# Attention scores on 32-row instead of 64-row TensorE tiles

## The chip, the cores and the metric

The kernel runs on one core of a Trainium2 chip. The metric is the device time of one execution in microseconds (us), the median of three runs.

## What is computed

For an input of 8 sequences with 1024 tokens of 128 channels the kernel normalizes each token (layer norm) and adds to the input an 8-head attention and a mixture of experts of the normalized tokens. In the attention a head has 2 query and key channels and 16 value channels:

```python
q = (x @ Wq.T + bq).reshape(B, M, H, dqk)      # dqk = 2
k = (x @ Wk.T + bk).reshape(B, M, H, dqk)
v = (x @ Wv.T + bv).reshape(B, M, H, dv)       # dv = 16
scores = jnp.einsum('bmhd,bnhd->bhmn', q, k) / math.sqrt(dqk)
scores = jnp.where(scores >= 0, scores, 0.2 * scores)
beta = jax.nn.softmax(scores, axis=-1)
out = jnp.einsum('bhmn,bnhd->bmhd', beta, v).reshape(B, M, C)
return gamma * out + x
```

The experts are 16 (12 of them two-layer networks with 512 hidden channels), with two chosen per token and a capacity of 1024 tokens each.

## The kernel before

The work has these stages on one core. First a prologue over 16 groups of 512 tokens (two of each sequence): statistics, normalizing, transposing, projecting to q, k, v and the router's logits, splitting q and k into three bfloat16 parts each (high, middle, low), and storing the parts to `parts_dram`. The groups are software-pipelined: each engine's program is a loop over steps, in which a step holds pieces of several groups. The parts lie in two buffers, so the copy of a group's high parts (line 674, ScalarE) waits until the stores of the group two before it have landed (`parts_out0`, `parts_out1`). Behind the last group VectorE ranks the tokens' experts. Then come attention on the first three sequences, the experts, and attention on the other five.

SP's queue in order: the loads of `x` (L261); eight DMAs of one row of -1 into `kz` (L269); twelve DMAs that clear `disp` (L272); for each group the stores of its parts (L281 once, L285 three times, L292 for a row of shifts); the operand loads of the first sequence (L312 to L314); and then, pass by pass, further operand loads and the moves of finished rows.

A score of one head is a product over 18 rows: 3 key parts times 3 query parts times 2 channels. The softmax is made safe by a bound, the shift, of each query; it is subtracted as one further row (query side: the shift; key side: -1). The raw product holds the 18 rows alone. VectorE rectifies it where it lies, in PSUM (L1133: maximum with 0, times 4), a second product, the shifted one, with the shift's row too, is added onto it there, and ScalarE takes the exponential to `pr` (L718).

A tile for one head pair has 64 rows: 18 for one head, 18 for the other head, zeros, and the two rows of ones at the end. `kz` holds the keys once for each of the two heads of a tile, with zeros in the other's rows; `q2` holds the queries of both. Two tiles, at rows 0 and 64, make the two heads of a unit.

Attention runs over 32 passes (sequence, group of 4 heads, half of the queries: 512), each of 16 units; a unit is 128 keys of two heads, so 1024 scores per partition in two PSUM banks. There are 512 units, and a ring of three such bank pairs. `unit_of` gives a unit its pass, block of keys (`kc`) and head pair. TensorE's order is written out by hand: for each unit i, `shifted(i)` (L835, waits for VectorE's rectification of i), `scores(i + 2)` (L825, the raw products, waits for the exponential of i - 1, which frees the ring's place), and `values` (L855), half of a value step, in four column tiles of 32. At each pass's sixth unit VectorE also transposes the last pass's result (L1109, L1115).

The changed names are `TILE`, `ONES` (the row of ones, and the rows of a raw product), `q2`, the row writes at L263 to L269, `load_operands` (L301 to L314), the clearing of `q2` (L397), `scores` and `shifted`.

Of the kernel before, what the change touches and what calls it, by code (L numbers as in the profile page):

```python
# [5 lines left out]
F32 = mybir.dt.float32  # L6
BF16 = mybir.dt.bfloat16
# [5 lines left out]
P = 128  # L13
B, M, C = 8, 1024, 128
# [3 lines left out]
H, DV, DQ = 8, 16, 2  # L18
HG = 4
NHG = H // HG  # L20
# [4 lines left out]
HALF = 512  # L25
# [3 lines left out]
PROWS = KROW + 3 * QP  # L29
NPROD = 3 * 3 * DQ  # L30
NROW = NPROD + 1
TILE = 64
ONES = TILE - 2
DIRS = 16
E, E_MLP, FFN = 16, 12, 512
FC = FFN // P
# [16 lines left out]
PAIRS = HG // 2  # L53
# [48 lines left out]
def build(nc, x, consts, w_qk, b_qk, w_vr, b_v, r_b, n_w, n_w_row, w1t, b1, w2t, b2, cvec, gamma, out):  # L102
    parts_dram = nc.dram_tensor("parts_dram", [2, NROW * H, T], BF16, kind="Internal").ap()
# [3 lines left out]
    with ExitStack() as ctx:  # L107
        def sb(name, shape, dt=F32):
            return ctx.enter_context(nc.sbuf_tensor(name, shape, dt))

        def sem(name):
            return ctx.enter_context(nc.semaphore(name))
# [33 lines left out]
        shift = sb("shift", [P, GW], BF16)  # L146

        kz = sb("kz", [P, NHG, PAIRS, M], BF16)
        q2 = sb("q2", [P, NHG, M], BF16)
        w1 = sb("w1", [P, 4 * FFN])  # L150
        vp = sb("vp", [P, NHG, TB, HG, 32])
        pr = sb("pr", [P, BUFS, HG, HALF])
# [4 lines left out]
        rowones = sb("rowones", [1, M], BF16)  # L157
# [48 lines left out]
        S = {n: sem(n) for n in names}  # L206
# [6 lines left out]
        def wait_done(engine, name, count):  # L213

            if not (isinstance(count, int) and count <= 0):
                engine.wait_ge(S[name], count)
# [22 lines left out]
        def unit_of(i):  # L239

            p, n = divmod(i, UP)
            return p, p // NQ % NHG, p % NQ, n // PAIRS, n % PAIRS
# [7 lines left out]
        def spreads(p):  # L250

            return sum(k not in LAST and k % 2 == p % 2 for k in range(p + 1))

        def pass_at(b, hg, qh):
            return (b * NHG + hg) * NQ + qh

# [2 lines left out]
        def _(sp):  # L259
# [3 lines left out]
            sp.wait_ge(S["init_rdy"], 1)  # L263
            sp.wait_ge(S["ztile"], 1)
            sp.wait_ge(S["qz_init"], 1)
            for hg in range(NHG):
                for g in range(HG):
                    r = TILE * (g // PAIRS) + ONES + g % PAIRS
                    sp.dma_start(kz[r:r + 1, hg, g % PAIRS, :], rowones[:]).then_inc(S["kz_init"], 16)  # L269

            for e in range(E_MLP):
                sp.dma_start(disp[e * CAP:(e + 1) * CAP, :].rearrange("(p j) c -> p (j c)", p=P),  # L272
# [23 lines left out]
            for u in range(2):  # L296
                sp.wait_ge(S[f"parts_out{u}"], 64 * B)
                sp.wait_ge(S[f"shift_out{u}"], 16 * B)
            sp.wait_ge(S["kz_init"], 16 * NHG * HG)

            def load_operands(b, hg):  # L301

                if b > 0:
                    sp.wait_ge(S["s2"], UP * (pass_at(b - 1, hg, NQ - 1) + 1))
                for g in range(HG):
                    h = hg * HG + g
                    tok = bass.ts(b, M)
                    krows = parts_dram[1, :, tok].rearrange("(r h) t -> h r t", h=H)[h]
                    qrows = parts_dram[0, :, tok].rearrange("(r h) t -> h r t", h=H)[h]
                    r = TILE * (g // PAIRS) + NPROD * (g % PAIRS)  # L310
                    o = TILE * (g // PAIRS) + ONES + g % PAIRS
                    sp.dma_start(kz[r:r + NPROD, hg, g % PAIRS, :], krows[0:NPROD, :]).then_inc(S[f"ld{hg}"], 16)  # L312
                    sp.dma_start(q2[r:r + NPROD, hg, :], qrows[0:NPROD, :]).then_inc(S[f"ld{hg}"], 16)
                    sp.dma_start(q2[o:o + 1, hg, :], qrows[NPROD:NROW, :]).then_inc(S[f"ld{hg}"], 16)  # L314

            def store_sequence(s):

# [18 lines left out]
            def operands_in(p):  # L336

                if p % NPB == 0 and p > 0:
                    load_operands(p // NPB, 1)
                if p % NPB == NQ and p // NPB + 1 < B:  # L340
                    load_operands(p // NPB + 1, 0)

            for hg in range(NHG):
                load_operands(0, hg)
# [45 lines left out]
        def _(pool):  # L390
# [3 lines left out]
            pool.memset(va[:, :, :, DV:DV1], 1.0)  # L394
            pool.memset(vp[:], 0.0).then_inc(S["init_rdy"], 1)
            pool.memset(kz[:].rearrange("p a e m -> p (a e m)").bitcast(F32), 0.0)
            pool.memset(q2[:].rearrange("p a m -> p (a m)").bitcast(F32), 0.0).then_inc(S["qz_init"], 1)  # L397

            def prologue(at):
                if at(1):  # L400
# [22 lines left out]
            def value_rows(b, hg):  # L423

                if b > 0:
                    pool.wait_ge(S["pv"], TB * (pass_at(b - 1, hg, NQ - 1) + 1))
                pool.tensor_copy(vp[:, hg, :, :, 0:DV1],
                                 va[:, bass.ts(b, TB), hg * HG:(hg + 1) * HG, :]).then_inc(S["vp_rdy"], 1)
# [339 lines left out]
        def _(pe):  # L768
# [42 lines left out]
            for n, (lhs, rhs) in enumerate(((cbf[:, C_TRI:C_TRI + P], cnt), (onesb[:], incl))):  # L811
                pe.wait_ge(S["cnt_rdy"], n + 1)
                for half in range(2):
                    last = pe.matmul(ps_acc[:, half, :], lhs, rhs[:, half * HALF:(half + 1) * HALF], start=(n == 0),
                                     stop=(n == 1))
            last.then_inc(S["pos_rdy"], 1)

            def scores(i):
                p, hg, qh, kc, pair = unit_of(i)
                if i % (NQ * UP) == 0:  # L820
                    pe.wait_ge(S[f"ld{hg}"], NLOAD * (p // NPB + 1))
                wait_done(pe, "exps", i - RING + 1)
                for k in range(2):
                    r = TILE * k
                    last = pe.matmul(ring[i % RING][:, k, :], kz[r:r + ONES, hg, pair, kc * P:(kc + 1) * P],  # L825
                                     q2[r:r + ONES, hg, qh * HALF:(qh + 1) * HALF], start=True, stop=True,
                                     tile_position=(r, 0))
                last.then_inc(S["s1"], 1)

            def shifted(i):  # L830
                p, hg, qh, kc, pair = unit_of(i)
                pe.wait_ge(S["relu"], i + 1)
                for k in range(2):
                    r = TILE * k
                    last = pe.matmul(ring[i % RING][:, k, :], kz[r:r + TILE, hg, pair, kc * P:(kc + 1) * P],  # L835
                                     q2[r:r + TILE, hg, qh * HALF:(qh + 1) * HALF], start=False, stop=True,
                                     tile_position=(r, 0), skip_group_check=True)
                last.then_inc(S["s2"], 1)

# [29 lines left out]
            def ahead(b, n):  # L869

                for i in range(b * NUB, b * NUB + n):
                    scores(i)

            def attention(b0, b1):
                first, end = b0 * NUB, b1 * NUB
                for i in range(first, end):
                    shifted(i)
                    if i + AHEAD < end and i != BH * NUB:
                        scores(i + AHEAD)
                    if i > first + PAIRS:  # L880
                        values((i - 3) // PAIRS, (i - 3) % PAIRS)
                values((end - 3) // PAIRS, (end - 3) % PAIRS)
                if b1 == BH:
                    pe.wait_ge(S["exps"], end - RING + 1)
                    turn_rows(0, 0)
                for j in range(end - 2, end):
                    values(j // PAIRS, j % PAIRS)
# [333 lines left out]
```

## Time and profile before

| | |
|---|---|
| device time, median of 3 runs | 941.46 us (941.45 to 942.2) |
| span of the profiled execution | 940.0 us |
| TensorE matmul busy | 861.2 us (92%) |
| VectorE busy | 735.3 us (78%) |
| ScalarE busy | 691.3 us (74%) |
| GpSimd busy | 601.5 us (64%) |
| attention, first three sequences | 127 to 362 us |
| experts | 362 to 543 us |
| attention, other five | 543 to 931 us |

The profile is of one execution; its span runs from the program's first to its last instruction, and the device time also holds what lies around it, some 1.5 us. A matmul's busy time includes the latency of its pipeline, so a full TensorE row isn't TensorE at its peak. Idle time of an engine is put down to what ended it.

### The profile page before, as it was taken

What the parts mean: (1) busy time and instruction counts of PE and PEld (TensorE: products, weight loads), DVE (VectorE), ACT (ScalarE), POOL (GpSimd) and SP (SyncE); (2) the same over time, 40 slices, a digit from 0 to 9 for tenths busy, and PEclk for the clock granted to TensorE, in tenths of its full rate; (3) what the DMA queues carried; (4) which work ended last, traced back from release to release, by engine and by line L of the source; (5) the groups of instructions that cost most, each with busy time, mean ns of one, the idle gap of its engine ahead of it and who ended that gap; (6) DMA issues with size and microseconds to landing.
All of it is one profiled execution on the core that took longest, in us unless ns stands there. A gap on an engine that the chain in (4) does not pass through costs nothing. (4 is left out here: it accounts for less than half of the span.)

```text
span 940.0 us, 20061 instructions
## 1 busy us (share of the span) xinstructions
PE 861.2 (92%) x7499; PEld 348.9 (37%) x7500; DVE 735.3 (78%) x859; ACT 691.3 (74%) x811; POOL 601.5 (64%) x610
## 2 busy tenths in 40 slices
PE   0688269999999999999999999999999999999997
PEld 0444112222222224776867732222222222222222
DVE  5788889999999994101011099999999999999996
ACT  0578888888888887444453568888888888888886
POOL 3355247777777663999999226657567575765782
PEclk9999659999999999999999999999999999999999
DMA  7833101111111112233242210102112111210202
GB/s 214 303 66 74 32 27 33 51 40 51 47 27 36 25 38 88 90 121 116 93 138 71 94 44 22 40 19 59 36 25 59 25 36 29 70 29 13 69 18 55
DMA packets 71225, 59.36 MB, mean 63 GB/s; under 512 B 33770, under 2 KB 58178, under 8 KB 71136
## 3 DMA queue, kind: packets, MB, share of 16 engines
q1 hardware_dynamic: 61520, 48.06, 17.6%
q0 software_dynamic: 8192, 9.37, 3.6%
q8 instruction: 55, 0.90, 0.4%
q10 hardware_dynamic: 1424, 0.76, 0.3%
q14 instruction: 34, 0.28, 0.1%
HBM read 31.58 MB, written 30.02 MB: 66 GB/s over the span
## 5 line engine op out<-in xcount | busy, mean ns | idle before, releaser
L1133 DVE TENSOR_SCALAR ps<-ps 128x1024 f32<-128x1024 f32 x512 | 600.1, 1224 | 14.6 <-PE ps L825 11.7
L718 ACT ACTIVATE pr<-ps 128x1024 f32<-128x1024 f32 x512 | 523.4, 1023 | 104.5 <-PE ps L835 72.9
L855 PE MATMUL ps<-pr,vp 128*32 128x256 f32 x4096 | 327.2, 392 | 0.1
L835 PE MATMUL ps<-q,kz 64*128 64x512 bf16 x1024 | 200.7, 389 | 10.2 <-DVE ps L1133 4.4
L825 PE MATMUL ps<-q,kz 62*128 62x512 bf16 x1024 | 200.3, 389 | 2.9 <-DMA q<-parts_dram 1.3
L505 POOL DMA_INDIRECT xs<-eout,idxs x128 | 129.0, 1008 | 105.0 <-ACT pr L718 75.5
L490 POOL DMA_INDIRECT disp<-xn,idx x128 | 125.9, 984 | 50.8 <-issue 29.2
L835 PEld LDWEIGHTS ps<-q,kz 64*128 64x128 bf16 x1024 | 49.0, 93 | 225.7 <-DVE ps L1133 188.4
L1152 DVE TENSOR_TENSOR pr<-ps,parts 128x1024 f32<-128x1024 f32 x12 | 14.7, 1225 | 149.6 <-PE ps L920 149.6
L855 PEld LDWEIGHTS ps<-pr,vp 128*32 128x32 f32 x4096 | 81.1, 108 | 119.4 <-issue 117.6
L744 ACT ACTIVATE pr<-ps,b1s 128x512 f32<-128x512 f32 x96 | 65.8, 687 | 53.7 <-PE ps L909 53.7
L920 PEld LDWEIGHTS ps<-w,pr 128*128 128x128 f32 x768 | 88.6, 192 | 6.2 <-issue 6.2
L920 PE MATMUL ps<-w,pr 128*128 128x128 f32 x768 | 89.8, 275 | 0.0
L825 PEld LDWEIGHTS ps<-q,kz 62*128 62x128 bf16 x1024 | 49.3, 93 | 107.1 <-ACT pr L718 76.3
L909 PE MATMUL ps<-pr,w 128*128 128x512 f32 x192 | 84.7, 593 | 0.0
L628 POOL TENSOR_TENSOR y<-y,xn x24 | 56.4, 2351 | 4.9 <-POOL xn L625 4.9
L525 POOL TENSOR_TENSOR y<-y,xs 128x256 f32<-128x256 f32 x64 | 46.5, 727 | 11.4 <-POOL y L525 5.7
L452 POOL TENSOR_TENSOR y<-y,moved 128x256 f32<-128x256 f32 x32 | 23.4, 731 | 45.1 <-DMA moved<-att 26.8
L909 PEld LDWEIGHTS ps<-pr,w 128*128 128x128 f32 x192 | 35.5, 190 | 40.2 <-issue 39.5
L404 POOL TENSOR_TENSOR ot<-pr,parts 112x512 f32<-112x512 f32 x16 | 18.7, 1170 | 38.1 <-ACT parts L674 38.0
L737 ACT ACTIVATE pr<-ps,nw 128x512 f32<-128x512 f32 x24 | 15.2, 683 | 37.4 <-PE ps L898 37.4
L518 POOL TENSOR_TENSOR xs<-xs,co 128x256 f32<-128x256 f32 x64 | 37.9, 618 | 0.6
(122 smaller groups left out, 530.3 us busy)
## 6 DMA issues: line engine op xcount, KB each, us to landing
moved<-att SPq DMA_DIRECT2D x480, 8.0 KB
disp<-pr SPq DMA_DIRECT2D x12, 512.0 KB, 4.9
eout<-pr SPq DMA_DIRECT2D x12, 512.0 KB, 2.9
y<-in_x SPq DMA_DIRECT2D x8, 512.0 KB, 8.1
out<-y SPq DMA_DIRECT2D x7, 512.0 KB
w<-in_w1t SPq DMA_DIRECT2D x12, 256.0 KB, 3.2
w<-in_w2t SPq DMA_DIRECT2D x12, 256.0 KB, 3.4
xs<-disp SPq DMA_DIRECT2D x6, 512.0 KB, 4.9
```

What stands on the lines that cost most here:

```text
L490: pool.indirect_dma_start(out=disp, out_offset=bass.IndirectOffsetOnAxis(ap=idx[:, k, s * TB + t:s * TB + t + 1], axis=0), in_=xn[:, s * T ...
L505: pool.indirect_dma_start(out=g1[:, g % 2, t, c, :], out_offset=None, in_=eout, in_offset=bass.IndirectOffsetOnAxis(ap=idxs[:, c, GB * i + ...
L525: pool.tensor_tensor(yt, yt, rows[:, :, c, :], ALU.add).then_inc(S["comb" if c else "weighted"], 1)
L628: pool.tensor_tensor(yb, yb, xb, ALU.add).then_inc(S["pool_step"], 1)
L718: act.activation(pr[:, c % BUFS, 2 * pair:2 * pair + 2, :], ring[i % RING], ACT.Exp, scale=SLOPE).then_inc(S["exps"], 1)
L744: act.activation(hs[:, f, half * HALF:(half + 1) * HALF], ps[:, 2 + n % 4, :], ACT.Gelu, bias=b1s[:, u, f:f + 1]).then_inc(S["gel"], 1)
L825: last = pe.matmul(ring[i % RING][:, k, :], kz[r:r + ONES, hg, pair, kc * P:(kc + 1) * P], q2[r:r + ONES, hg, qh * HALF:(qh + 1) * HALF], ...
L835: last = pe.matmul(ring[i % RING][:, k, :], kz[r:r + TILE, hg, pair, kc * P:(kc + 1) * P], q2[r:r + TILE, hg, qh * HALF:(qh + 1) * HALF], ...
L855: last = pe.matmul(acc[p % 2][32 * g:32 * g + 32, cols], vp[:, hg, kc, g, :], pr[:, c % BUFS, g % PAIRS * 2 + g // PAIRS, cols], start=(kc ...
L909: pe.matmul(ps[:, 2 + n % 4, :], w1[:, 2 * u * FFN + f * P:2 * u * FFN + (f + 1) * P], dt_[:, half * HALF:(half + 1) * HALF], start=True, ...
L920: mm = pe.matmul(o, hs[:, f, j * P:(j + 1) * P], w1[:, (2 * u + 1) * FFN + f * P:(2 * u + 1) * FFN + (f + 1) * P], start=(f == 0), stop=(f ...
L1133: dve.tensor_scalar(s, s, 0.0, 1.0 / SLOPE - 1.0, ALU.max, ALU.mult).then_inc(S["relu"], 1)
```

## The change

Each head gets a tile of its own, of 32 rows: 18 rows, 13 rows of zeros, and the row of ones at the end. Four tiles fill the 128 rows: two sets of two. Both sets hold the same operands, the keys and queries of all four heads of the group, a head pair behind the other in the free dimension (so `q2` has a further dimension, of twice the size). A unit with an even block of keys uses the tiles at rows 0 and 32, one with an odd block those at 64 and 96. As a block has two units, unit i + 2 uses the other set than unit i.

The rows of ones are written by 16 DMAs instead of 8. The operand loads are 12 DMAs per sequence and head group as before; each now brings two heads, and each is made for both sets. `shifted` takes all 32 rows, `scores` the first 31. The order of instructions on TensorE stays.

```diff
--- before.py
+++ after.py
@@ -29,8 +29,9 @@
 PROWS = KROW + 3 * QP
 NPROD = 3 * 3 * DQ
 NROW = NPROD + 1
-TILE = 64
-ONES = TILE - 2
+TILE = 32
+ONES = TILE - 1
+SETS = 2
 DIRS = 16
 E, E_MLP, FFN = 16, 12, 512
 FC = FFN // P
@@ -146,7 +147,7 @@
         shift = sb("shift", [P, GW], BF16)
 
         kz = sb("kz", [P, NHG, PAIRS, M], BF16)
-        q2 = sb("q2", [P, NHG, M], BF16)
+        q2 = sb("q2", [P, NHG, PAIRS, M], BF16)
         w1 = sb("w1", [P, 4 * FFN])
         vp = sb("vp", [P, NHG, TB, HG, 32])
         pr = sb("pr", [P, BUFS, HG, HALF])
@@ -251,6 +252,10 @@
 
             return sum(k not in LAST and k % 2 == p % 2 for k in range(p + 1))
 
+        def rows_of(z, k):
+
+            return TILE * (2 * z + k)
+
         def pass_at(b, hg, qh):
             return (b * NHG + hg) * NQ + qh
 
@@ -263,10 +268,12 @@
             sp.wait_ge(S["init_rdy"], 1)
             sp.wait_ge(S["ztile"], 1)
             sp.wait_ge(S["qz_init"], 1)
-            for hg in range(NHG):
-                for g in range(HG):
-                    r = TILE * (g // PAIRS) + ONES + g % PAIRS
-                    sp.dma_start(kz[r:r + 1, hg, g % PAIRS, :], rowones[:]).then_inc(S["kz_init"], 16)
+            for z in range(SETS):
+                for k in range(2):
+                    r = rows_of(z, k) + ONES
+                    for hg in range(NHG):
+                        for pair in range(PAIRS):
+                            sp.dma_start(kz[r:r + 1, hg, pair, :], rowones[:]).then_inc(S["kz_init"], 16)
 
             for e in range(E_MLP):
                 sp.dma_start(disp[e * CAP:(e + 1) * CAP, :].rearrange("(p j) c -> p (j c)", p=P),
@@ -296,22 +303,22 @@
             for u in range(2):
                 sp.wait_ge(S[f"parts_out{u}"], 64 * B)
                 sp.wait_ge(S[f"shift_out{u}"], 16 * B)
-            sp.wait_ge(S["kz_init"], 16 * NHG * HG)
+            sp.wait_ge(S["kz_init"], 16 * NHG * SETS * HG)
 
             def load_operands(b, hg):
 
                 if b > 0:
                     sp.wait_ge(S["s2"], UP * (pass_at(b - 1, hg, NQ - 1) + 1))
-                for g in range(HG):
-                    h = hg * HG + g
-                    tok = bass.ts(b, M)
-                    krows = parts_dram[1, :, tok].rearrange("(r h) t -> h r t", h=H)[h]
-                    qrows = parts_dram[0, :, tok].rearrange("(r h) t -> h r t", h=H)[h]
-                    r = TILE * (g // PAIRS) + NPROD * (g % PAIRS)
-                    o = TILE * (g // PAIRS) + ONES + g % PAIRS
-                    sp.dma_start(kz[r:r + NPROD, hg, g % PAIRS, :], krows[0:NPROD, :]).then_inc(S[f"ld{hg}"], 16)
-                    sp.dma_start(q2[r:r + NPROD, hg, :], qrows[0:NPROD, :]).then_inc(S[f"ld{hg}"], 16)
-                    sp.dma_start(q2[o:o + 1, hg, :], qrows[NPROD:NROW, :]).then_inc(S[f"ld{hg}"], 16)
+                tok = bass.ts(b, M)
+                for k in range(2):
+                    heads = slice(hg * HG + k * PAIRS, hg * HG + (k + 1) * PAIRS)
+                    krows = parts_dram[1, :, tok].rearrange("(r h) t -> r h t", h=H)[:, heads, :]
+                    qrows = parts_dram[0, :, tok].rearrange("(r h) t -> r h t", h=H)[:, heads, :]
+                    for z in range(SETS):
+                        r = rows_of(z, k)
+                        sp.dma_start(kz[r:r + NPROD, hg, :, :], krows[0:NPROD]).then_inc(S[f"ld{hg}"], 16)
+                        sp.dma_start(q2[r:r + NPROD, hg, :, :], qrows[0:NPROD]).then_inc(S[f"ld{hg}"], 16)
+                        sp.dma_start(q2[r + ONES:r + TILE, hg, :, :], qrows[NPROD:NROW]).then_inc(S[f"ld{hg}"], 16)
 
             def store_sequence(s):
 
@@ -394,7 +401,7 @@
             pool.memset(va[:, :, :, DV:DV1], 1.0)
             pool.memset(vp[:], 0.0).then_inc(S["init_rdy"], 1)
             pool.memset(kz[:].rearrange("p a e m -> p (a e m)").bitcast(F32), 0.0)
-            pool.memset(q2[:].rearrange("p a m -> p (a m)").bitcast(F32), 0.0).then_inc(S["qz_init"], 1)
+            pool.memset(q2[:].rearrange("p a e m -> p (a e m)").bitcast(F32), 0.0).then_inc(S["qz_init"], 1)
 
             def prologue(at):
                 if at(1):
@@ -821,9 +828,9 @@
                     pe.wait_ge(S[f"ld{hg}"], NLOAD * (p // NPB + 1))
                 wait_done(pe, "exps", i - RING + 1)
                 for k in range(2):
-                    r = TILE * k
+                    r = rows_of(kc % SETS, k)
                     last = pe.matmul(ring[i % RING][:, k, :], kz[r:r + ONES, hg, pair, kc * P:(kc + 1) * P],
-                                     q2[r:r + ONES, hg, qh * HALF:(qh + 1) * HALF], start=True, stop=True,
+                                     q2[r:r + ONES, hg, pair, qh * HALF:(qh + 1) * HALF], start=True, stop=True,
                                      tile_position=(r, 0))
                 last.then_inc(S["s1"], 1)
 
@@ -831,9 +838,9 @@
                 p, hg, qh, kc, pair = unit_of(i)
                 pe.wait_ge(S["relu"], i + 1)
                 for k in range(2):
-                    r = TILE * k
+                    r = rows_of(kc % SETS, k)
                     last = pe.matmul(ring[i % RING][:, k, :], kz[r:r + TILE, hg, pair, kc * P:(kc + 1) * P],
-                                     q2[r:r + TILE, hg, qh * HALF:(qh + 1) * HALF], start=False, stop=True,
+                                     q2[r:r + TILE, hg, pair, qh * HALF:(qh + 1) * HALF], start=False, stop=True,
                                      tile_position=(r, 0), skip_group_check=True)
                 last.then_inc(S["s2"], 1)
```

## Rows read from the trace of the kernel before

**Rows 1.** Busy us by stage, PE to POOL (x instructions), PEclk, DMA share, GB/s.
```profile
600.00:900.00 300.00, 297.14 (x2972) 86.36 (x2964) 298.66 (x278) 252.87 (x248) 195.27 (x247) 1.00 0.15 39
```

**Rows 2.** The page's groups: line, shapes, count | busy, mean ns | idle before.
```profile
L855 PE MATMUL ps<-pr,vp 128*32 128x256 f32 x4096 | 327.2, 392 | 0.1
L835 PE MATMUL ps<-q,kz 64*128 64x512 bf16 x1024 | 200.7, 389 | 10.2 <-DVE ps L1133 4.4
```

**Rows 3.** Waits by name, whole span: us in total, times, longest us.
```profile
PEld ps L825 <- ACT pr L718: 76.3, 307, 1.4
```

**Rows 4.** Timeline of TensorE: start us, us, line, tiles, count; two units of attention.
```profile
702.23 0.39 PE L835 MATMUL ps<-q,kz 64*128 64x512 bf16 x2
702.57 0.39 PE L825 MATMUL ps<-q,kz 62*128 62x512 bf16 x2
702.89 0.64 PE L855 MATMUL ps<-pr,vp 128*32 128x256 f32 x8
703.46 0.39 PE L835 MATMUL ps<-q,kz 64*128 64x512 bf16 x2
703.75 0.39 PE L825 MATMUL ps<-q,kz 62*128 62x512 bf16 x2
```

**Rows 5.** Timeline of ScalarE, same stretch.
```profile
701.49 1.02 ACT L718 ACTIVATE pr<-ps 128x1024 f32<-128x1024 f32 x1 [0.20 <-PE ps L835]
702.67 1.02 ACT L718 ACTIVATE pr<-ps 128x1024 f32<-128x1024 f32 x1 [0.15 <-PE ps L835]
```

**Rows 6.** Timeline of VectorE over one pass, with its turns.
```profile
704.14 0.71 DVE L1109 STREAM_TRANSPOSE ot<-ps 128x512 f32<-128x512 f32 x1
723.53 0.71 DVE L1109 STREAM_TRANSPOSE ot<-ps 128x512 f32<-128x512 f32 x1
724.16 1.20 DVE L1133 TENSOR_SCALAR ps<-ps 128x1024 f32<-128x1024 f32 x1
725.42 5.72 DVE L1133 TENSOR_SCALAR ps<-ps 128x1024 f32<-128x1024 f32 x5
```

**Rows 7.** Line 269 on SP: duration ns min/median/max, first, last start.
```profile
L269 SPq DMA_DIRECT2D kz<-rowones x8: 578/589/1516, 16.3 to 21.7; - x8
```

**Rows 8.** DMA of line 272, its last issue at 33.9 us.
```profile
DMA to landing us min/median/max: 5.2/5.2/5.2
```

**Rows 9.** DMAs of line 285, the first group's stores.
```profile
L285 SPq DMA_DIRECT2D parts_dram<-parts x3: 425/466/642, 37.2 to 38.4; - x3
DMA to landing us min/median/max: 2.0/2.2/2.5
```

**Rows 10.** Timeline of ScalarE ahead of attention: line 674, third and sixth group.
```profile
40.91 0.62 ACT L674 CAST parts<-pr 112x512 bf16<-112x512 f32 x1
53.57 0.62 ACT L674 CAST parts<-pr 112x512 bf16<-112x512 f32 x1 [1.16 <-DMA parts_dram<-parts]
```

**Rows 11.** Timeline of TensorE ahead of attention and in its first units.
```profile
29.71 2.05 PE L785 MATMUL ps<-pr,wqk 128*112 128x512 f32 x2 [0.76 <-ACT pr L686]
42.79 1.11 PE L785 MATMUL ps<-pr,wqk 128*112 128x512 f32 x2 [0.67 <-ACT pr L686]
...
102.79 1.44 PE L806 MATMUL ps<-parts,cbf 112*128 112x512 bf16 x3 [4.65 <-DVE hat L1009]
123.78 1.04 PE L825 MATMUL ps<-q,kz 62*128 62x512 bf16 x4 [1.33 <-DMA q<-parts_dram]
134.20 0.61 PE L835 MATMUL ps<-q,kz 64*128 64x512 bf16 x2
134.60 0.64 PE L825 MATMUL ps<-q,kz 62*128 62x512 bf16 x2
136.18 0.57 PE L835 MATMUL ps<-q,kz 64*128 64x512 bf16 x2
```

**Rows 12.** Busy time by stage again, from the prologue's end into attention.
```profile
102.00:137.00 35.00, 13.43 (x57) 2.50 (x62) 31.99 (x32) 30.84 (x69) 8.29 (x20) 0.51 0.10 25
```

**Rows 13.** Timeline of VectorE, its first units of attention.
```profile
127.15 3.59 DVE L1133 TENSOR_SCALAR ps<-ps 128x1024 f32<-128x1024 f32 x3
```

## The prediction

> **What bounds the kernel now.** I read the stages first: through an attention stage VectorE is busy 298.66 of 300 us and TensorE 297.14 at full clock [rows 1]. Both look full, so busy shares don't decide, and I went to the order inside one unit (one of 512: 128 keys, 512 queries, two heads). TensorE repeats three steps: the shifted pair of unit i (L835), the raw pair of unit i+2 (L825), half of a value step (L855) [rows 4]. ScalarE runs one exponential per unit [rows 5]. The reader is to see what starts L825: an exponential begun at 701.49 ends at 702.51, and L825 starts at 702.57; the next ends at 703.69, and L825 starts at 703.75. The waits by name say the same: weight loads of L825 waited for L718 307 times [rows 3].
>
> So the pace is a loop over two units. From one exponential's end: 0.06 to L825, 0.32 to L855 (702.57 to 702.89), 0.57 to L835 (to 703.46), 0.44 from L835 to its exponential (702.23 to 702.67), 1.02 for the exponential itself. That is 2.41 us for two units, 1.20 per unit. VectorE alone would be a little quicker: after a turn it makes five units in 5.72 us, with 1.20 for the last, so (5.72 - 1.20) / 4 = 1.13 per unit [rows 6]. A pass of 16 units also holds a turn, which costs 0.63 (723.53 to 724.16) and 0.13 more one unit later (1.26 instead of 1.13). Its floor is 16 x 1.13 + 0.76 = 18.84 us; it takes 19.39 (704.14 to 723.53), the 16 x 1.20 = 19.2 of the loop and a rest in which VectorE's turn delays TensorE.
>
> The stage ahead of attention is a chain of steps over 16 groups, followed by routing on VectorE. It has no clock time that it waits for, so whatever delays one step moves the end.
>
> **Part 1: the overlap of raw and shifted products.** Before, both pairs use all four row groups, so L825 can't start while L835 streams in. After, they use different ones, and four banks. But L825 follows L835 by 0.28 to 0.34 us [rows 4], and in each case what ends that gap is the exponential of unit i-1 [rows 5]. In the loop above no term is a raw pair that waits for a shifted pair. When L825 starts with the exponential's end as now, L855 follows it by the same 0.32, since its column tiles need the whole array as before. Only behind a turn, where VectorE is late, are the exponentials ready and the gap between the pairs, 0.28 at most, would go; but there the next L835 waits for VectorE, and the values simply end earlier. Gain: 0.
>
> What could be non-zero is the length of the loop's three TensorE terms with 32 rows. The trace of before has no such tile. Nearest rows: 389 ns for 64 rows and 392 for 128 rows [rows 2], so rows hardly count; I take 0, and as bounds 3 ns either way in each of three terms, 9 ns per two units, 256 x 9 ns = 2.3 us either way.
>
> The skill speaks for the change here. The Trainium skill, TensorE: Matmul & The Clock Gate, Part 3, gives 3.07x for four row tiles of 32 rows against one after the other. By that rule the two pairs would take the time of one, and the sum would hold a saving for each unit; the row above shows no wait there to save.
>
> **Part 2: first units of attention.** They run at the lower clock: 0.51 over 102 to 137 us, that is 1.2 GHz [rows 12]. There TensorE is late: L825 starts 0.40 after L835 (134.20, 134.60) [rows 11], with the exponential already done. About two units pass before the clock is back; the overlap gives at most 2 x 0.40 = 0.8. One of the two still waits for an exponential for part of it: I take -0.5, bounds 0 and -0.8.
>
> **Part 3: eight more ones-row DMAs on SP's queue.** The ones rows of kz are written by 16 DMAs instead of 8. Each holds the queue for 0.589 plus some 0.04 to the next; eight more take 8 x 0.63 = 5.06 us (5.99/8 x 8 = 6.0 if the slow first one, 1.516, were the rule) [rows 7]. Behind them on the same queue come, in this order, the 12 fills of `disp` with zeros (L272) and then the stores of the q and k parts (L281, L285). All twelve fills move by 5.06. The last lands at 33.9 + 5.2 = 39.1 now [rows 8], so at 44.2 after. The first group's stores, issued from 37.2 to 38.4, land 2.0 after the last issue, at 40.4, just behind the fills [rows 9]; I take them to stay behind them, at 40.4 + 5.06 = 45.5.
>
> Who waits for that: ScalarE's copy of the third group's high parts (L674) overwrites the first group's buffer. It starts at 40.91 now, with half a us to spare, and without a wait [rows 10]. After, it can't start before 45.5: a stall of 4.55 us. Everything else of ScalarE stands behind it in order (value rows, the next transposed block), so TensorE and VectorE starve, and the whole chain to attention moves by as much. One thing is given back: three groups later the same line waited 1.16 us for a DMA (53.57) [rows 10], a slow store issue; shifted work may hide that. Half of it, -0.6; bounds 0 and -1.16.
>
> A consequence: TensorE now idles 0.67 ahead of that step's successor (42.79); with the stall it idles 0.67 + 4.55 = 5.2 us. Its clock fell in the one place where it idled 4.65 us (to 102.79) [rows 11, 12]. At the lower clock the two q/k products of a group took 2.05 us (29.71) instead of 1.11 (42.79), and the first group shows that the value products behind them double too, so a step grows by about 2 us, for one step or two. Bounds 0 (the clock holds) and +4; I take +1.4, nearer to one step with a fall that isn't certain.
>
> **Part 4: more bytes and zeros.** The operand loads stay 12 DMAs per group of heads, each of two heads, and are made twice: double the bytes. For the first, TensorE waits (1.33, to 123.78) [rows 11], but VectorE takes up the first unit only at 127.15, right behind the routing [rows 13]; with 0.6 us of raw product at the low clock, 2.7 us of later landing stay hidden. What exceeds that costs one for one; I estimate under 1 us more, since the queue issues as many DMAs as before. Later loads have a pass or more to land. Clearing the doubled `q2` is POOL's, long before SP comes to the rows. All at 0.
>
> **Sum.** 4.55 - 0.6 + 1.4 - 0.5 + 0 = +4.85 us. The profiled execution spans 940.0, and the three timed runs have the median 941.46, so 1.5 lies around the span; I take the sum onto the median: 946.3. With all bounds: 4.55 - 1.16 - 0.8 - 2.3 = +0.3 and 4.55 + 4 + 2.3 = +10.9, or +11.8 by the higher price per DMA.
>
> **Rivals.**
> - *Faster: the loop opens.* If raw pairs on their own row groups pull the whole unit forward, so that the two-unit loop falls under VectorE's pace, each pass falls from 19.39 to 18.84: 32 x 0.55 = 17.6 us less, with part 3 paid 928 to 934. It decides from the point where L825 no longer starts 0.06 behind an exponential. Against it: three slots of the ring force that wait, and the change leaves them. The rule of the Trainium skill named above would end here. Chance 0.10.
> - *Same: the late queue is absorbed.* If the stores pass the fills, or the 1.16 and the start both come back in full and the clock holds, +0.3 to +1.8: 941.5 to 943.2. For it: half a us of spare time already, and one later stall. Against it: nothing in the chain can work ahead. Chance 0.15.
> - *Much slower: the clock stays low.* Overlapped products make TensorE's activity sparser in the first units; if the clock then stays at 1.2 GHz, the loop is 0.06, then 1.58 from L825 to the next L835 (134.60 to 136.18), 0.66 to the exponential (a pair takes 0.61 there, 0.22 more than 0.39), 1.02: 3.32, or 1.66 a unit, and the 190 units of the first three sequences cost 190 x 0.46 = 87 us: 1030. Against it: at that clock the loop leaves TensorE only 0.06 of 1.66 idle after a raw pair, and at full clock nothing gets sparser, as nothing overlaps. Chance 0.06.
> - *Slower by the loop:* 32-row tiles that cost 20 ns or more per unit, over 10 us on top: 955 to 960. Chance 0.05.
>
> **How the numbers follow.** The forecast (late queue, loop unchanged) has 0.64: 943.3 to 951. The range of 8 in 10 takes this and the same-case: 941 to 951. A measurement of this kernel tells about 0.2%, 1.9 us, from no change. Faster by more: the first rival and a trace of short loops, 0.12. Same: 0.15. Slower: 0.73.
>
> **What would show it.** Right: L269 x16, about 11 us of SP's queue; the third L674 at 45 us with a wait for the stores; VectorE's first rectification at 130 to 133 instead of 127.15; a pass still of 19.4 us, with L825 0.06 behind an exponential. Wrong: a pass near 18.9 (the loop opened); L674 unshifted (stores overtook the fills, part 3 falls); granted clock 0.5 beyond the first units of attention.

## The result, and the profile after

The changed kernel takes 948.06 us (median of four runs, 945.64 to 948.57), the kernel before 941.83 in the runs taken with it (941.45 to 942.86): a ratio of 1.0059, with a 95% interval of 1.0042 to 1.0077. It is slower by 0.6%, inside the range of 941 to 951, where +4.85 us were forecast: +6.2 between the medians, +5.8 between the spans of the profiled executions (945.8 and 940.0). Line numbers behind the constants lie 5 to 7 higher than before: L261 is L266, L825 is L832, L835 is L842, L855 is L862, L1133 is L1140. In the experiments' kernels they differ by a few lines again; the raw pair is told by its 31 or 62 rows, the shifted one by 32 or 64.

SP's queue first (start, duration, line, count; two lines of before, then four of the changed kernel). The ones rows now hold it for 11.06 us, and everything behind them is late:

```profile
22.33 12.72 SPq L272 DMA_DIRECT2D disp<-pr  x12
36.86 0.33 SPq L281 DMA_DIRECT2D parts_dram<-parts  x1
...
16.16 11.06 SPq L276 DMA_DIRECT2D kz<-rowones  x16
27.26 12.76 SPq L279 DMA_DIRECT2D disp<-pr  x12
40.07 1.21 SPq L288 DMA_DIRECT2D parts_dram<-parts  x1
41.32 2.44 SPq L292 DMA_DIRECT2D parts_dram<-parts  x3
```

The fills begin at 27.26, 4.93 later than before, and the first store goes out at 40.07, right behind them, where it went out at 36.86. What that does to ScalarE's copy of the high parts (L674 before, L681 now), for the third to the sixth group, is in its timeline; the brackets give idle time and what ended it:

```profile
45.26 0.62 ACT L681 CAST parts<-pr 112x512 bf16<-112x512 f32 x1 [4.60 <-DMA parts_dram<-parts]
...
50.04 0.62 ACT L681 CAST parts<-pr 112x512 bf16<-112x512 f32 x1
...
54.36 0.62 ACT L681 CAST parts<-pr 112x512 bf16<-112x512 f32 x1
...
58.21 0.62 ACT L681 CAST parts<-pr 112x512 bf16<-112x512 f32 x1
```

The third group's copy waits 4.60 us for the stores and starts at 45.26, where it had started at 40.91 without a wait [rows 10]; the sixth group's copy waits for nothing now, at 58.21, where it had waited 1.16 us. TensorE stands idle behind the first of these, and its next product takes 2.05 us, not 1.11 [rows 11]:

```profile
47.15 2.05 PE L792 MATMUL ps<-pr,wqk 128*112 128x512 f32 x2 [5.23 <-ACT pr L693]
```

Busy time by stage (PE, PEld, DVE, ACT, POOL with their instruction counts, granted clock, DMA share, GB/s) says why: 0.50 of the clock, 1.2 GHz, over the six us around the end of the stall and behind it. The second row is the start of the second attention stage, where the clock falls once more; the third is the same stretch in the kernel before, at 1.00:

```profile
44.00:50.00 6.00, 2.85 (x7) 1.79 (x8) 3.21 (x11) 3.10 (x6) 2.31 (x2) 0.50 0.34 81
550.00:560.00 10.00, 8.32 (x64) 1.97 (x61) 8.19 (x7) 7.06 (x8) 2.29 (x3) 0.66 0.39 123
550.00:560.00 10.00, 10.00 (x106) 2.95 (x104) 10.00 (x10) 8.53 (x9) 3.09 (x3) 1.00 0.10 29
```

VectorE's timeline gives the sum of this: its first unit of attention comes at 132.00, 4.85 us later than before [rows 13], and a pass, from turn to turn, takes 729.76 - 710.40 = 19.36 us, where it took 19.39 [rows 6].

```profile
132.00 3.48 DVE L1140 TENSOR_SCALAR ps<-ps 128x1024 f32<-128x1024 f32 x3
...
710.40 0.70 DVE L1116 STREAM_TRANSPOSE ot<-ps 128x512 f32<-128x512 f32 x1
...
729.76 0.70 DVE L1116 STREAM_TRANSPOSE ot<-ps 128x512 f32<-128x512 f32 x1
```

In the steady state TensorE's and ScalarE's timelines look as before [rows 4, 5]. The two exponentials in the second fence follow each other: the first runs from 707.75 to 708.77, and L832 starts at 708.83; the second ends at 709.94, and L832 starts at 710.00. L832 lies 0.28 to 0.34 behind L842, as it did, although the two no longer share a row group:

```profile
708.49 0.39 PE L842 MATMUL ps<-q,kz 32*128 32x512 bf16 x2
708.83 0.39 PE L832 MATMUL ps<-q,kz 31*128 31x512 bf16 x2
...
709.72 0.39 PE L842 MATMUL ps<-q,kz 32*128 32x512 bf16 x2
710.00 0.39 PE L832 MATMUL ps<-q,kz 31*128 31x512 bf16 x2
```

```profile
707.75 2.19 ACT L725 ACTIVATE pr<-ps 128x1024 f32<-128x1024 f32 x2 [0.20 <-PE ps L842]
```

So the path of the 5.8 us, by the start of the same unit in both traces: +4.85 at the first unit of attention, +4.38 at the last of the first stage (unit 191: 364.88 against 360.50), +4.97 behind the experts (unit 192: 545.80 against 540.83), +6.45 twelve units on (unit 204), behind the second fall of the clock, and +6.0 at the last unit (936.1 against 930.1).

### The profile page after: what moved, and what is told of

The parts are those of the page before. It is cut to its first block, busy times and chain, and to the rows that moved or that the text cites. A ratio compares the mean times of both kernels' runs of the same rounds, so it can differ in the third digit from the quotient of the medians.

```text
span 945.8 us, 20070 instructions
## 1 busy us (share of the span) xinstructions
PE 860.7 (91%) x7500; PEld 348.3 (37%) x7500; DVE 734.4 (78%) x859; ACT 691.4 (73%) x811; POOL 601.8 (64%) x610
## 4 chain that ended last, share of the span: by engine, by line
PE 61%; DVE 23%; ACT 5%; issue 5%; DMA 2%; SPq 2%; POOL 1%; POOLq 0%; DVEq 0%; ACTq 0%
DVE ps L1140 19%; PE ps L862 18%; PE ps L842 11%; PE ps L832 11%; PE ps L927 9%; PE ps L916 8%; ACT y L703 2%; DVE ot L1116 2%; PE ps L792 1%; PE ps L905 1%; ACT pr L725 1%; DMA y<-in_x 1%; DMA pr<-disp 1%; DVE bst L975 1%; SPq L266 1%
## 5 line engine op out<-in xcount | busy, mean ns | idle before, releaser
L1140 DVE TENSOR_SCALAR ps<-ps 128x1024 f32<-128x1024 f32 x512 | 599.7, 1223 | 15.8 <-PE ps L832 13.1
L862 PE MATMUL ps<-pr,vp 128*32 128x256 f32 x4096 | 329.5, 394 | 0.1
L842 PE MATMUL ps<-q,kz 32*128 32x512 bf16 x1024 | 200.8, 389 | 10.4 <-DVE ps L1140 5.8
L832 PE MATMUL ps<-q,kz 31*128 31x512 bf16 x1024 | 200.7, 390 | 5.7 <-DMA q<-parts_dram 3.6
L842 PEld LDWEIGHTS ps<-q,kz 32*128 32x128 bf16 x1024 | 48.1, 91 | 227.4 <-DVE ps L1140 183.4
L862 PEld LDWEIGHTS ps<-pr,vp 128*32 128x32 f32 x4096 | 81.3, 108 | 117.8 <-issue 116.0
L832 PEld LDWEIGHTS ps<-q,kz 31*128 31x128 bf16 x1024 | 48.3, 91 | 109.3 <-ACT pr L725 80.0
```

The lines of the kernel that those rows point to most:

```text
L862: last = pe.matmul(acc[p % 2][32 * g:32 * g + 32, cols], vp[:, hg, kc, g, :], pr[:, c % BUFS, g % PAIRS * 2 + g // PAIRS, cols], start=(kc ...
L1140: dve.tensor_scalar(s, s, 0.0, 1.0 / SLOPE - 1.0, ALU.max, ALU.mult).then_inc(S["relu"], 1)
```

## Experiments

**1. The ones rows in 4 DMAs instead of 16.** One DMA per tile, with a source that is repeated over head groups and pairs.

```diff
-                    for hg in range(NHG):
-                        for pair in range(PAIRS):
-                            sp.dma_start(kz[r:r + 1, hg, pair, :], rowones[:]).then_inc(S["kz_init"], 16)
+                    sp.dma_start(kz[r:r + 1, :, :, :].rearrange("p a e m -> p (a e) m"),
+                                 rowones[:].unsqueeze(1).broadcast_to([1, NHG * PAIRS, M])).then_inc(S["kz_init"], 16)
...
-            sp.wait_ge(S["kz_init"], 16 * NHG * SETS * HG)
+            sp.wait_ge(S["kz_init"], 16 * 2 * SETS)
```

> The changed kernel, with its ones rows written by 4 DMAs (one per tile, with all head groups and pairs) in place of 16. Theory (the late queue of SP makes the loss, the tiles themselves are neutral): the fills and stores are no later than in the kernel before, the third group's copy (L674 of before) waits for no store, TensorE's clock holds there, VectorE's first rectification comes at 127 to 128 us instead of 132.0, and the time is 941 to 943.5 us, the upper end if the clock falls again at the start of the second attention stage (552 us in the changed kernel, 1.7 us there). Rival (the tiles cost time in attention): the start comes back, but the time stays at 945 or more. Rival (the overlap is worth something, hidden by the late queue): 938 or less.

Measured: 941.96 us (940.98 to 943.25, ten runs) against 941.0; ratio 1.0003, 0.9991 to 1.0016. The loss is gone, to within that interval of -0.8 to +1.5 us. ScalarE's third copy starts at 40.86 without a wait, and the sixth group's wait is back (0.95, to 53.31), as before the change:

```profile
40.86 0.62 ACT L680 CAST parts<-pr 112x512 bf16<-112x512 f32 x1
```

So 32-row tiles and doubled loads make no difference that these runs can tell, and the 0.6% is the queue's. One thing stayed: in the profiled execution the clock fell at the start of the second attention stage here too, as it had in the changed kernel:

```profile
550.00:560.00 10.00, 10.00 (x86) 2.50 (x84) 8.56 (x8) 6.95 (x8) 3.13 (x4) 0.69 0.19 57
```

The first units of attention, at 1.2 GHz, are where the pairs do overlap. In TensorE's timeline both start at 134.69, the next unit follows 1.56 us later, where it took 1.98 without overlap (134.20 to 136.18 [rows 11]), and there the clock is back (0.43 for a pair instead of 0.61):

```profile
134.69 0.61 PE L841 MATMUL ps<-q,kz 32*128 32x512 bf16 x2
134.69 0.61 PE L831 MATMUL ps<-q,kz 31*128 31x512 bf16 x2
...
136.25 0.43 PE L841 MATMUL ps<-q,kz 32*128 32x512 bf16 x2
```

By VectorE's starts 0.6 us were gained over the first sixteen units: +0.69 against before at unit 0, +0.05 at unit 16. That this is the overlap's isn't shown: experiment 2, on 64-row tiles and without overlap, gains 0.5 there (+5.84 to +5.30). How long the clock stays low in these units differs from one execution to the next.

**2. The kernel before, with 8 more ones-row DMAs.** The mirror of it: 64-row tiles, and eight more DMAs into a spare tile that nobody reads.

```diff
+        spare = sb("spare", [NHG * HG, M], BF16)
...
                     sp.dma_start(kz[r:r + 1, hg, g % PAIRS, :], rowones[:]).then_inc(S["kz_init"], 16)
+                    o = HG * hg + g
+                    sp.dma_start(spare[o:o + 1, :], rowones[:]).then_inc(S["kz_init"], 16)
...
-            sp.wait_ge(S["kz_init"], 16 * NHG * HG)
+            sp.wait_ge(S["kz_init"], 16 * NHG * HG * 2)
```

> The kernel before, with 8 more DMAs of the same row of ones into a spare tile, each behind one of the 8 that are there; tiles and products as before. Theory: the queue alone makes the loss: fills 5.06 us later, the third group's copy near 45.3 us with a wait of about 4.6 us, the first rectification 4.9 us later, a time of 946 to 948 us. Rival (the tiles or the doubled loads make the loss): 942 us.

Measured: 948.19 us (946.7 to 948.72), ratio 1.0063, 1.0043 to 1.0084. The whole loss, without the change's tiles. The third copy came at 45.49; its wait is shorter, as the copy of the group before it had itself come a microsecond later in this execution (38.08 instead of 37.06):

```profile
45.49 0.62 ACT L677 CAST parts<-pr 112x512 bf16<-112x512 f32 x1 [3.10 <-DMA parts_dram<-parts]
```

The first unit of attention stands 5.84 us behind that of the kernel before, 1.0 more than in the changed kernel. Of this 0.2 was there at the third copy, and 0.7 came by the fifth (55.25 against 54.36): over 50 to 54 us the granted clock was 0.69 here and 0.91 in the changed kernel.

The granted clock fell behind the stall here too (0.64 over 44 to 50 us), and at the second stage's start:

```profile
550.00:560.00 10.00, 8.31 (x66) 2.31 (x64) 7.62 (x8) 6.55 (x7) 2.30 (x3) 0.83 0.29 93
```

So a fall at 550 us is no mark of the 32-row tiles alone. It is shorter here: (1 - 0.83) / 0.5 x 10 = 3.4 us of 10, against (1 - 0.66) / 0.5 x 10 = 6.8 in the changed kernel.

**3. One set of tiles for all units.** Experiment 1, but no two products in flight can use different row groups of the two sets.

```diff
-                    r = rows_of(kc % SETS, k)
+                    r = rows_of(0, k)
```

(in `scores` and in `shifted`.)

> The first experiment's kernel (4 DMAs for the ones rows), with every unit on the tiles at rows 0 and 32, so that raw and shifted products can't overlap; both sets are still loaded. Theory (in the steady state nothing overlaps, because a raw product starts behind an exponential): a pass stays at 19.35 to 19.4 us, and the time is within 1 us of the first experiment, later by at most the 0.5 us of the first units at the lower clock. Rival (the overlap is worth the gap between the pairs, 0.28 us, in every unit or every second): a pass of 21.6 to 24, slower by 70 us or more; even in one unit of a pass: 9 us.

Measured: 1329.53 us (1328.06 to 1330.18), ratio 1.41. The theory fell, and the rival did not happen as it was written either: a unit takes 1.98 us, by the pace of L841 in TensorE's timeline, every step of it at the lower clock.

```profile
302.05 0.61 PE L841 MATMUL ps<-q,kz 32*128 32x512 bf16 x2
302.45 0.63 PE L831 MATMUL ps<-q,kz 31*128 31x512 bf16 x2
...
304.03 0.61 PE L841 MATMUL ps<-q,kz 32*128 32x512 bf16 x2
```

The raw pair starts 0.40 behind the shifted one, where it had started together with it at this clock in experiment 1. The stages show the clock. Through both attention stages TensorE has no gap in its busy time (200.00 of 200) and is granted 0.50, 1.2 GHz; the experts in between run at 1.00. So the second stage began at the full clock, lost it some 8 us in, as other kernels do (see below), and did not get it back.

```profile
150.00:350.00 200.00, 200.00 (x1216) 33.67 (x1212) 129.03 (x113) 103.32 (x101) 93.52 (x96) 0.50 0.11 31
540.00:680.00 140.00, 140.00 (x817) 102.93 (x816) 12.24 (x10) 63.94 (x95) 117.49 (x54) 1.00 0.34 109
700.00:900.00 200.00, 200.00 (x1216) 33.75 (x1216) 129.07 (x114) 103.40 (x102) 72.71 (x91) 0.50 0.10 26
```

**4. A shorter value step, on the kernel before.** Exponentials and value rows in bfloat16; the attention weights are rounded more coarsely.

```diff
-        vp = sb("vp", [P, NHG, TB, HG, 32])
+        vp = sb("vp", [P, NHG, TB, HG, 32], BF16)
...
-                act.activation(pr[:, c % BUFS, 2 * pair:2 * pair + 2, :], ring[i % RING], ACT.Exp, scale=SLOPE
+                act.activation(pr16[:, c % BUFS, 2 * pair:2 * pair + 2, :], ring[i % RING], ACT.Exp, scale=SLOPE
...
-                                     pr[:, c % BUFS, g % PAIRS * 2 + g // PAIRS, cols],
+                                     pr16[:, c % BUFS, g % PAIRS * 2 + g // PAIRS, cols],
```

(`pr16` is a bfloat16 view of the first half of `pr`; the last two lines are in `values`.)

> The kernel before, with the exponentials and value rows kept in bfloat16, so that a value step takes one pass through the array in place of two; the products of scores are as before. It rounds the attention weights more coarsely. Theory (a loop over two units of exponential, raw pair, values, shifted pair sets the pace): the term from L855 to the next L835 falls from 0.57 to about 0.2 to 0.25, the loop from 2.41 to about 2.05 us, under VectorE's 2 x 1.13, so VectorE becomes the bound: a pass of 18.85 to 18.95 instead of 19.39, 14 to 17 us less, 924 to 928 us. Rival (VectorE sets the pace already): a pass of 19.3 to 19.4 and 941 us.

Measured: 924.13 us (923.19 to 924.91), ratio 0.9815, 0.979 to 0.984. From L858 (a value step) to the next L838 it is 0.43 us now, and TensorE starts a unit every 1.13:

```profile
301.06 0.29 PE L858 MATMUL ps<-pr,vp 128*32 128x256 bf16 x4
301.49 0.39 PE L838 MATMUL ps<-q,kz 64*128 64x512 bf16 x2
301.87 0.39 PE L828 MATMUL ps<-q,kz 62*128 62x512 bf16 x2
```

The value step's own products are four instead of eight. The shifted pair now starts 0.05 behind VectorE's rectification of its unit (which ends at 301.44), so that 0.43 holds a wait. VectorE's turns lie 18.84 us apart (322.45 - 303.61), the floor that the prediction worked out for it:

```profile
303.61 0.70 DVE L1112 STREAM_TRANSPOSE ot<-ps 128x512 f32<-128x512 f32 x1
...
322.45 0.70 DVE L1112 STREAM_TRANSPOSE ot<-ps 128x512 f32<-128x512 f32 x1
```

Of the 28 passes 20 take 18.83 or 18.84; the other eight, 19.11 to 19.24, are those in which the granted clock falls for a while. Yet L828 still starts 0.06 behind an exponential: two of them run from 299.66 to 301.81, and L828 starts at 301.87.

```profile
299.66 2.15 ACT L721 ACTIVATE pr<-ps 128x1024 bf16<-128x1024 f32 x2
```

So that distance, by which the prediction meant to tell whether the loop has opened, doesn't tell it; the length of a pass does.

This beats both kernels, on 64-row tiles, at the price of the coarser rounding.

**5. Two sets, but chosen by the head pair.** Units i and i + 2 then share a set. All four row groups are used, in turn, and raw and shifted products can't overlap; again in both functions.

```diff
-                    r = rows_of(kc % SETS, k)
+                    r = rows_of(pair, k)
```

> The first experiment's kernel, with the set of tiles chosen by the head pair instead of the block of keys. Units i and i + 2 then share a set, so raw and shifted products can't overlap, but all four row groups are used in turn. It tells two readings of the one-set run (1329 us at half clock) apart. Theory (TensorE's clock comes back only when the 32-row products of two sets run at the same time, so that more rows are in use at once): clock at 1.2 GHz through both attention stages, a unit of 1.98 us, 1320 to 1335 us. Rival (it is enough that all rows are used over time): the clock comes back a few units into attention, a pass of 19.4 us, 941 to 944 us.

Measured: 1328.7 us (1328.14 to 1329.9), as with one set, and by the same pace: the raw pair 0.40 behind the shifted one, and TensorE busy for 200.00 of the 200 us from 150 to 350 at a granted 0.50.

```profile
300.45 0.60 PE L841 MATMUL ps<-q,kz 32*128 32x512 bf16 x2
300.85 0.63 PE L831 MATMUL ps<-q,kz 31*128 31x512 bf16 x2
```

It is thus not enough that all rows are used in turn: the clock came back where the pairs could overlap and stayed low where they could not. How the overlap acts on the clock no run shows. With 64-row tiles it came back without any overlap (134.20 to 136.18 [rows 11]).

**6. The shorter value step on 32-row tiles.** Experiments 1 and 4 together.

> The first experiment's kernel (32-row tiles, 4 DMAs for the ones rows) with exponentials and value rows in bfloat16, as in the fourth experiment on 64-row tiles (924.1 us, mean clock 0.964, short falls of the clock here and there). It rounds the attention weights more coarsely. Theory (32-row products use fewer of TensorE's rows at a time, so its clock falls more easily once the value step is short as well): a mean clock below 0.96, and at least 10 us over the fourth experiment, up to 1085 us if the clock stays low in attention, at some 1.43 us a unit. Rival (tiles of 32 and 64 rows are worth the same to the clock as long as raw and shifted products may overlap): 923 to 926 us.

Measured: 993.83 us (991.07 to 994.29), ratio 1.053, mean clock 0.643: 70 us over the same step on 64-row tiles. The theory held; a unit takes 1.32 us on average (a pass 21.01 to 21.09), less than the 1.43 by which its upper end was reckoned. A pair takes 0.61, as at the lower clock:

```profile
300.78 0.61 PE L844 MATMUL ps<-q,kz 32*128 32x512 bf16 x2
301.32 0.61 PE L834 MATMUL ps<-q,kz 31*128 31x512 bf16 x2
...
302.20 0.61 PE L844 MATMUL ps<-q,kz 32*128 32x512 bf16 x2
302.50 0.61 PE L834 MATMUL ps<-q,kz 31*128 31x512 bf16 x2
```

```profile
150.00:350.00 200.00, 196.50 (x1218) 48.02 (x1214) 190.91 (x173) 155.61 (x152) 139.97 (x144) 0.50 0.16 44
```

So 32-row tiles, neutral with the long value step, lose the clock where that step is short, although the pairs may overlap: L834 lies 0.54 behind L844 in one unit (300.78 to 301.32) and 0.30 in the next (302.20 to 302.50), and in three units of four the distance is 0.39 or more. A raw pair that has to wait for the shifted one follows it by 0.40 at this clock (experiment 3), so there is next to no overlap.

**7. The ones rows behind the fills.** The changed kernel, with the order of the two blocks on SP's queue exchanged.

> The changed kernel with its 16 ones-row DMAs issued behind the twelve fills instead of ahead of them; nothing else differs. It separates the two things that the late queue did: the first group's stores are issued late either way (near 40.4 us), but the fills are out of their way (landed by 33 us). Theory (both count): the stores' last landing near 43.9 instead of 45.2, so a wait of the third group's copy of 3.1 to 3.3 us instead of 4.60, and a time 1 to 2.5 us under the changed kernel, 945.5 to 947. Rival (the fills in flight don't count): a wait of 4.5 us and the changed kernel's 948. Rival (only the fills count): no wait and 942.

Measured: 947.36 us (945.34 to 947.95), ratio 1.0053, 1.0034 to 1.0072. The copy starts at 44.05, 1.2 us earlier than the changed kernel's 45.26, as was expected (43.9 instead of 45.2). The wait is 3.77, longer than the 3.1 to 3.3 expected, because the step ahead of it came 0.4 us earlier in this execution (39.50 instead of 39.89).

```profile
44.05 0.62 ACT L681 CAST parts<-pr 112x512 bf16<-112x512 f32 x1 [3.77 <-DMA parts_dram<-parts]
```

On SP's queue the first group's four stores go out even later than in the changed kernel (40.53 against 40.07), but take 2.0 us there (to 42.53) instead of 3.7 (to 43.76):

```profile
40.53 0.58 SPq L288 DMA_DIRECT2D parts_dram<-parts  x1
41.16 1.37 SPq L292 DMA_DIRECT2D parts_dram<-parts  x3
```

So most of the delay, 3.1 of 4.35 us at the copy (44.05 against 40.91 before), is the late queue alone, and 1.2 comes with the fills right ahead of the stores; whether by their data in flight or by their place in the queue this can't tell. The difference in time to the changed kernel, 0.7 us, is too small to tell from none.

## Why the prediction was right, and where it was not

**Bound and part 1.** The loop over two units was the right reading: shorten one term, and a pass falls to VectorE's floor, 18.84 (experiment 4). A rival that the prediction doesn't name is that TensorE is simply full. The trace of before speaks against it: at the shortest L825 follows L835 by 0.22 (138.77 to 138.99), and 0.22 + 0.32 + 0.57 = 1.11 us a unit is less than the 1.20 of the loop. The overlap's gain of 0 holds at 2.4 GHz: a pass gained 0.03 us. The rule of the Trainium skill (TensorE: Matmul & The Clock Gate, Part 3: four row tiles at 3.07x) bought nothing there, as the row said, since no pair waited for the other. The length of a product stayed too: 389 and 390 ns with 32 and 31 rows, 389 with 64. The row it was taken from, 389 against 392, compares products of another type and width, so it gave less support than it seemed to.

**The rival of the clock had its mechanism the wrong way round.** By it the overlap makes TensorE's work sparser, so that the clock stays low; chance 0.06. The runs show the opposite. Where the pairs overlap the clock came back (the changed kernel, experiment 1), and where they can't it stayed low in both attention stages, for some 387 us more (experiments 3 and 5), against the 87 reckoned for overlapping pairs (a unit of 1.98 instead of 1.66, and both stages instead of one). The sum has no term for this price of 32-row products; it gave the overlap 0.5 us, by the length of the first units alone. So that the changed kernel kept its clock was forecast, but not for the reason that the runs show.

**Part 2.** -0.5 forecast. Of the 4.85 at the first unit 4.65 were left at unit 16, so -0.2, and 4.38 at the end of the stage, a little of it from each pass. A unit at the lower clock did get shorter, 1.56 for 1.98 in experiment 1. But the lower clock lasted longer here: over the 15 us from VectorE's first unit on the granted clock was 0.64 in the changed kernel, 0.69 before, 0.72 and 0.73 in experiments 1 and 2. What the overlap alone is worth can't be told from this.

**Part 3.** The fills began 4.93 later, for 5.06 by the sum. The stall was 4.55 by the sum and 4.60 in the trace, and the copy came 4.35 later. The clock behind it fell: +1.4 taken; the copies of the fourth and fifth group came 5.29 and 5.76 later than before, so +1.41. That these agree is luck: 1.4 was weighed between 0 and 4, and by the same reckoning it was 2.1 in experiment 2 (4.58 to 6.65). The copies of the fourth and fifth group before:

```profile
44.75 0.62 ACT L674 CAST parts<-pr 112x512 bf16<-112x512 f32 x1
48.60 0.62 ACT L674 CAST parts<-pr 112x512 bf16<-112x512 f32 x1
```

Given back at the sixth group: 0.6 taken, half of a whole; it was the whole, 5.76 - 4.64 = 1.12. The sum at attention's start, 5.35 by the terms of part 3, was 4.85; that the whole forecast is +4.85 as well is chance. Experiments 1 and 2 show the queue as the cause from both sides.

**Part 4.** "Under 1 us" for the doubled first load was too little. SP's issues grew, against what was assumed: with two heads' rows per DMA the key rows mostly took 0.42 us instead of 0.27 and the shift rows 0.54 to 0.63 instead of 0.25. The twelve issues took 5.7 us (123.64 to 129.36) instead of 3.8 (118.79 to 122.61). First and last of them on SP's queue before, then first, a later and last in the changed kernel (start and duration):

```profile
118.79 0.27 SPq L312 DMA_DIRECT2D kz<-parts_dram  x1
...
122.35 0.26 SPq L314 DMA_DIRECT2D q<-parts_dram  x1
...
123.64 0.28 SPq L319 DMA_DIRECT2D kz<-parts_dram  x1
...
127.95 0.42 SPq L319 DMA_DIRECT2D kz<-parts_dram  x1
...
128.82 0.54 SPq L321 DMA_DIRECT2D q<-parts_dram  x1
```

TensorE's first raw pair came at 130.87, 7.09 later than before's 123.78, so 2.24 behind the shift of 4.85; 1.9 of that is SP's issuing. The cover of 2.7 held, with less than half a us left.

**Not foreseen.** The clock's fall at the second stage's start cost 1.7 us (4.75 at unit 195, 6.45 at unit 204). In the timeline the pairs overlap there too (554.61 and 554.68), and the next unit follows 1.62 us on (556.23):

```profile
554.61 0.61 PE L842 MATMUL ps<-q,kz 32*128 32x512 bf16 x2
554.68 0.61 PE L832 MATMUL ps<-q,kz 31*128 31x512 bf16 x2
```

It is no accident of one execution. Over the 15 us from the start of the second stage's first unit on, the granted clock was 0.74 to 0.80 in the profiles of all six kernels with 32-row tiles, 0.77 in the changed kernel and in experiments 1 and 7. Of the three with 64-row tiles two had 1.00 (before, experiment 4), and experiment 2 had 0.89. The mean clocks of whole executions fit: 0.975 to 0.979 in the ten of experiment 1 (median 0.9765), and 0.978 to 0.982 in the 14 of the kernel before taken with them (median 0.981); a fall of 6.8 us takes 0.0036 off such a mean. So in these runs the fall comes more often and lasts longer with 32-row tiles; why, no run shows. A granted clock of 0.5 beyond the first units was one of the prediction's signs of being wrong, and for this stretch it was seen. Behind the experts stand another +0.6, which experiments 1 (0.8) and 2 (0.56) have too and none of the steps explains; that stays open.

**The number.** +4.85 was forecast and +5.8 came, span against span. What was missed partly cancels: the whole return of 1.12 instead of 0.6, and the 0.03 of each pass, against 0.3 less in the first units, 1.7 for the second fall of the clock and the 0.6 behind the experts. That the sum came so near is in part luck; that the queue's delay carries it is not.

## What to carry to other kernels

Before two products are made to overlap, look at what starts the second one: if it is another engine's result, the gap between them isn't the first one's. Then count the set-up instructions that the new layout adds to an in-order queue and follow that queue to the first one who waits; eight DMAs of 0.6 us cost the whole loss here, and four DMAs with a repeated source in place of the sixteen took it back. And read the granted clock beside the busy share: a TensorE that is busy all the time can still be granted half.

## What the runs showed of the hardware

The clock did not follow the busy time of the profile: TensorE was busy for 200.00 of 200 us at a granted 0.50 with 32-row pairs one behind the other (experiments 3 and 5). With 64-row pairs, which have the same durations at each clock (0.61 and 0.39), it came back to 1.00 within a few units, and so it did with 32-row pairs that overlap. Once back it held 1.00 in the changed kernel's steady state, although the pairs there start 0.28 to 0.34 apart. A DMA of a single 2 KB row from one partition of SBUF to another held SP's queue for 0.589 us, more than twice as long as one of a 2 KB row from DRAM (0.25).
